# The attention's output projection as three products of split operands, and 18 identity turns in the prologue's waits

## The reference

```
x = x + tanh(g_xattn) * xattn(layernorm(x), ctx, ctx)
x = x + tanh(g_ffn)   * ffn(layernorm(x))

xattn: Q, K, V = x Wq' + bq, ctx Wk' + bk, ctx Wv' + bv      (16 heads of 16)
       out = softmax(Q K' / 4) V, heads side by side (100 x 256)
       return out Wh' + bh
ffn:   rmsnorm, softmax gate over 8 experts, the best 2, SwiGLU of width 1024
       with low-rank deltas of rank 16 for each expert
```

## Time and profile before

| | |
|---|---|
| three timed runs | 498.75, 499.56, 500.44 us; median 499.56 |
| profiled execution | 499.88 us, its span 498.0 us, mean granted clock of TensorE 0.995 |
| TensorE (PE) busy | 97% of the span |
| VectorE (DVE) / ScalarE (ACT) / GpSimd (POOL) busy | 72% / 53% / 56% |
| load of `wh` | issued at 34.2 us, landed 6.3 us later |
| queries of the second chunk split (what `q_l` = 6 counts) | 23.35 us |
| first score head of image 3 | about 69.8 us |
| loads of queries, issue to landing (median) | 3.3 us |
| VectorE, copy of 400 columns out of PSUM (L950) / difference of 400 columns, one operand in PSUM (L884) | 0.57 us / 0.574 us |

### The profile page before, as it was taken

The page is one execution under the profiler, slowest core; times in us unless marked ns, Lnnn a source line. Parts: engine busy times, 40 slices in busy tenths (PEclk is TensorE's granted clock), DMA queues, the critical chain, the costliest instruction groups (busy, mean ns, idle before and its releaser), DMA issues.

```text
span 498.0 us, 11753 instructions
## 1 busy us (share of the span) xinstructions
PE 482.1 (97%) x4350; PEld 454.2 (91%) x4350; DVE 358.4 (72%) x771; ACT 265.7 (53%) x584; POOL 276.9 (56%) x336
## 2 busy tenths in 40 slices
PE   7888999999999999999999999999999999999996
PEld 6657999999999999998999998899999999999994
DVE  5866787888888888988797779745585566764444
ACT  4466766666777766669865532533325333333331
POOL 6545665666666677685434547544485435845440
PEclk9989999999999999999999999999999999999999
DMA  7693786678777676554260000010000100001001
GB/s 214 176 291 98 219 208 163 153 183 195 199 184 180 174 188 158 121 111 79 50 185 1 1 0 2 1 34 1 0 2 0 34 1 1 0 2 34 0 1 33
DMA packets 51144, 45.83 MB, mean 92 GB/s; under 512 B 33935, under 2 KB 40115, under 8 KB 51088
## 3 DMA queue, kind: packets, MB, share of 16 engines
q1 hardware_dynamic: 41310, 23.18, 19.8%
q0 software_dynamic: 7504, 18.69, 14.0%
q10 hardware_dynamic: 2274, 3.21, 2.0%
HBM read 20.59 MB, written 6.66 MB: 55 GB/s over the span
## 4 chain that ended last, share of the span: by engine, by line
PE 90%; DVE 5%; DMA 2%; issue 1%; ACT 1%; SPq 0%; DVEq 0%; ACTq 0%
PE bank L1426 14%; PE bank L1270 9%; PE bank L1293 8%; PE bank L1306 7%; PE bank L1430 7%; PE bank L1443 7%; PE bank L1478 6%; PE bank L1252 6%; PE bank L1240 6%; PE bank L1458 4%; PE bank L1339 3%; PE bank L1461 2%; PE bank L1227 2%; DMA xs<-x 2%; PE bank L1386 2%; PE bank L1318 1%
## 5 line engine op out<-in xcount | busy, mean ns | idle before, releaser
L985 DVE TENSOR_REDUCE nmax<-bank 100x1 f32<-100x361 f32 x256 | 131.1, 530 | 34.0 <-PE bank L1270 29.7
L419 POOL TENSOR_TENSOR awl<-hb,awh 128x400 fp32r<-128x400 f32 x63 | 71.4, 1134 | 119.5 <-ACT awh L623 119.5
L623 ACT ACTIVATE awh<-hb 128x400 fp32r<-128x400 f32 x64 | 34.5, 538 | 118.4 <-DVE hb L921 118.1
L525 ACT ACTIVATE pt<-bank 120x400 f32<-120x400 f32 (+1 forms) x192 | 90.1, 501 | 12.6 <-PE bank L1293 9.5
L1270 PE MATMUL bank<-KS,QS 96*100 96x362 f32 x256 | 86.3, 357 | 3.7 <-DVE nmax L985 2.9
L914 DVE TENSOR_TENSOR hb<-sil,bank 128x400 f32<-128x400 f32 x64 | 36.4, 569 | 71.2 <-PE bank L1443 36.7
L1293 PE MATMUL bank<-QS,KS 97*120 97x200 f32 (+1 forms) x384 | 63.6, 269 | 0.0
L328 POOL TENSOR_TENSOR cth<-craw,cth 128x724 fp32r<-128x724 f32 x16 | 27.7, 1730 | 59.9 <-ACT cth L471 53.6
L1293 PEld LDWEIGHTS bank<-QS,KS 97*120 97x120 f32 (+1 forms) x384 | 59.2, 184 | 0.2
L1270 PEld LDWEIGHTS bank<-KS,QS 96*100 96x100 f32 x256 | 41.6, 167 | 9.6 <-DVE nmax L985 3.3
L333 POOL DMA_DIRECT2D QS<-q_dram x90 | 46.1, 521 | 0.4 <-issue 0.3
(11 more groups left out here) (225 smaller groups left out, 1117.1 us busy)
## 6 DMA issues: line engine op xcount, KB each, us to landing
KS<-kn SPq DMA_DIRECT2D x128, 90.5 KB, 3.3
KS<-kn POOLq DMA_DIRECT2D x64, 90.5 KB, 3.5
craw<-ctxT POOLq DMA_DIRECT2D x14, 361.0 KB, 5.0
QS<-q_dram POOLq DMA_DIRECT2D x92, 50.0 KB, 3.3
q_dram<-qn ACTq DMA_DIRECT2D x4, 400.0 KB, 4.4
o_dram<-on SPq DMA_DIRECT2D x16, 100.0 KB
xr<-o_dram SPq DMA_DIRECT2D x16, 100.0 KB
y<-xs SPq DMA_DIRECT2D x8, 200.0 KB
```

Source lines behind the costliest of these rows:

```text
L419: nc.gpsimd.tensor_tensor(awl[:, g % 2, slot], hb[:, slot], awh[:, g % 2, slot].bitcast(F32), ALU.subtract).then_inc(m["p_awl"], 1)
L525: nc.scalar.activation(pt[0:TW[t], u, :], pT[u % 3][0:TW[t], 0:CS], ACT.Exp, scale=float(DH) ** -0.5).then_inc(m["act_e"], 1)
L985: nc.vector.tensor_reduce(nmax[:, h // 8, pos % 8:pos % 8 + 1], pS[h % 2][0:S, 0:T], AX.X, ALU.max, negate=True).then_inc(m["dve_s"], 1)
```

## The change

The output projection becomes six matmuls of split operands. Its weight is split once, at the end of step 0 (ScalarE the high part, GpSimd the low part); the turned attention output is split each time, the high part by ScalarE (`turned_high`), the low part by VectorE in the place of the copy. In the prologue TensorE turns the identity 18 times at five places, into a bank that `q_proj` overwrites.

```
+        whs = sba("whs", [128, 2, KT, D], F32R)
...
-        ot = sba("ot", [128, KT, S])
+        ots = sba("ots", [128, 2, KT, S], F32R)
...
+                if i == 0:
+                    pool.wait_ge(m["wh_h"], 1)
+                    nc.gpsimd.tensor_tensor(whs[:, 1], wh[:], whs[:, 0].bitcast(F32), ALU.subtract).then_inc(m["wh_l"], 1)
...
+            def turned_high(i):
+                act.wait_ge(m["pe_onT"], i)
+                wait(act, "pe_y", i - 1)
+                nc.scalar.activation(ots[:, 0].rearrange("p k s -> p (k s)"), pP[1][:, 0:KT * S], ACT.Copy).then_inc(m["act_ot"], 1)
...
                 v_out(b, 1)
+                if has_y(i):
+                    turned_high(i)
                 expo(i, 8)
...
                     ctx_high_of(i + 3)
                 if i == 0:
+                    act.wait_ge(m["w_in"], 2 * 16)
+                    nc.scalar.activation(whs[:, 0], wh[:], ACT.Copy).then_inc(m["wh_h"], 1)
                     q_store(2)
...
                 expo(B - 2, 6)
+                turned_high(B - 2)
                 expo(B - 2, 7)
...
                 u_high(0, 0)
+                turned_high(B - 1)
                 u_high(0, 1)
...
                     slot_high(g, 0)
+                if g < 2:
+                    turned_high(B + g)
                 slot_high(g, 1)
...
             def turned_o(i):
-                dve.wait_ge(m["pe_onT"], i)
-                nc.vector.tensor_copy(ot[:].rearrange("p k s -> p (k s)"), pP[1][:, 0:KT * S]).then_inc(m["dve_ot"], 1)
+                dve.wait_ge(m["act_ot"], i)
+                nc.vector.tensor_tensor(ots[:, 1].rearrange("p k s -> p (k s)"), pP[1][:, 0:KT * S],
+                                        ots[:, 0].rearrange("p k s -> p (k s)").bitcast(F32), ALU.subtract).then_inc(m["dve_ot"], 1)
...
             def y_proj(i):
                 wait(pe, "dve_ot", i)
                 if i == 1:
-                    pe.wait_ge(m["w_in"], 2 * 16)
-                for k in range(KT):
-                    last = mm(pP[1][0:S, 0:D], ot[:, k, :], wh[:, k, :], start=k == 0, stop=k == KT - 1)
+                    pe.wait_ge(m["wh_l"], 1)
+                for p in range(3 * KT):
+                    (ho, hw), k = TERMS[p // KT], p % KT
+                    last = mm(pP[1][0:S, 0:D], ots[:, ho, k, :], whs[:, hw, k, :], start=p == 0, stop=p == 5)
                 last.then_inc(m["pe_y"], 1)
...
+            def keep_warm(n):
+                pe.wait_ge(m["q_l"], 3 * KT)
+                for _ in range(n):
+                    nc.tensor.transpose(pT[0][:, 0:128], ident[:], ident[:])
...
             k_proj(1, 0)
+            keep_warm(3)
             s_head(0, 2)
             s_head(0, 3)
             pe.wait_ge(m["dve_kl"], 2)
             k_proj(1, 1)
             s_head(0, 4)
+            keep_warm(4)
             s_head(0, 5)
+            keep_warm(4)
             s_head(0, 6)
+            keep_warm(3)
             turn(4)
             turn(5)
+            keep_warm(4)
             s_head(0, 7)
             q_proj(2, 0)
```

More of the change, by code:

```diff
@@ L187, in program @@
                  "fw_in fw2_in iota_ok erow_s erow_ok tgf_ok g0 g1 nw a_w p_w a_tx pe_t1 a_tth d_ttl pe_g d_lg d_max d_idx d_dm d_ix d_w silu_ok a_th "
-                 "nm_ok pe_u a_uh d_ul pe_ix d_mk p_md pe_w d_wb d_u0 p_u1 pe_h1 pe_h3 a_sil d_hb d_aw a_awh p_awl d_aws a_sh p_sl d_al "
+                 "nm_ok wh_h wh_l act_ot pe_u a_uh d_ul pe_ix d_mk p_md pe_w d_wb d_u0 p_u1 pe_h1 pe_h3 a_sil d_hb d_aw a_awh p_awl d_aws a_sh p_sl d_al "
                  "pe_z d_zt d_zm pe_fy pe_b2 a_fo d_fo pe_out f_out").split()
```

## The result

The changed kernel took 497.18 us (median of 20 executions, 496.33 to 499.39) against 499.45 us (20, 498.08 to 502.34) for the kernel before on the same chip. The ratio is 0.9954, 95% interval 0.9941 to 0.9966: faster by 0.46%. The forecast was 496.6 us, range 495.2 to 498.2. The profiled execution took 496.79 us (span 495.0, mean granted clock 0.999), the one before 499.88 (498.0, 0.995).

What follows compares the result with a forecast made beforehand. The prediction took TensorE, busy 97% of the span, and its clock as the bound. 499.88 - 2.4 (projections) - 1.62 (clock) + 0.22 (turns) + 0.5 (hand-over) = 496.6 us, range 495.2 to 498.2.

Steps and rivals of the forecast that it cites:

- Three products for one: Output projections: six split matmuls take 0.72 us instead of 0.86, 17 times, a gain of 2.4 us.
- Column time: Rival, output projections: six split matmuls take only their columns' time, 0.64 us, 1.3 us less in all, 495.3 us; chance 0.08.
- the four instructions' own price: Bound for the output projections: at 0.215 us each, six matmuls take 1.29 us, a loss of 7.3 us.
- another engine bounds the step: Rival, attention steps: the projections shrink but the gain is lost in a new wait, 499.0 us; chance 0.08.
- High part, low part, halves of `wh`: Operand splits in attention steps, weight split at end of step 0: covered, cost nothing; uncovered 3.2 us (high part), 1.9 (`wh`).
- The hand-over where it is tight: Last attention step and first expert group: the low part, waiting for ScalarE, comes late; +0.2 and +0.3, together +0.5 us.
- The turns: Prologue: 18 turns of 0.109 us, 1.96 us in all, fifteen of them inside TensorE's waits; cost +0.22 us.
- three turns are uncovered, +0.22 us: Prologue: the first three turns delay `k_proj(1, 1)` by 0.33 us and with it ScalarE's `k_high`; +0.22 us.
- The clock: Prologue, 29.40 to 32.80 us: turns hold TensorE's clock, `q_proj(2, 0)` takes 1.38 us instead of 3.00; a gain of 1.62 us.
- no gain from the clock: Rival, prologue: timed runs had no clock loss, or it falls still or elsewhere; only projections count, 497.9 us; chance 0.27.
- The idle stretch is the program's, not chance: Argument against the clock rival: TensorE's idle stretch in the prologue ahead of the fall belongs to the program; no size given.

Runs made afterwards that it cites:

- four-matmul kernel: Changed kernel with four of each output projection's six matmuls, leaving out high part by the weights' low half: 495.10 us, ratio 0.9886 to the kernel before.
- kernel before with early store: Kernel before, with the store of `on` to memory issued behind the second group of key stacks instead of the last: 499.93 us, ratio 0.9996.

## Why the prediction was right, and where its sizes were off

**Three products for one: right.** 0.72 us as the value projection's row said, 17 times. Column time (0.64 for six) is refuted by 102 matmuls, and so is the four instructions' own price. The Trainium skill, "TensorE: Matmul & The Clock Gate", section "Back-to-back issue gap", would have 0.65 for six by columns / 2.4 GHz + 2.5 ns. It gives that gap for an isolated matmul, and says that with a load of weights for every matmul it is too little at few columns and too much at 512. This case's 0.12 us for one, each with its own load, stands above the rule's 0.109. The term, 2.4 us, counted all 17 as taken from the path. One was not: the step of about 200 us is VectorE's, and lasts 13.3 us with six, with four, and with the old ones. That is the rival "another engine bounds the step", true in one step for the 0.14 us. Behind it the distances shrink by 0.12, 0.17, 0.15 and 0.03 us (14.09, 9.93, 9.47 and 13.78 before, 13.97, 9.76, 9.32 and 13.75 with the change, in the two executions named below), and the four-matmul kernel shows that there was little more to be had there.

**High part, low part, halves of `wh`: right.** 0.33 and 0.35 us, both covered; the steps shrink by what the projection does (13.24 to 13.10 in the undisturbed ones). No wait of TensorE for a load of queries or keys stands between 50 and 80 us in a profiled execution with GpSimd's part.

**The hand-over where it is tight: right in place, about right in size.** Predicted +0.5. VectorE's rows of the last attention step and of the first expert group:

```profile
242.46 0.37 DVE L988 TENSOR_TENSOR ots<-bank,ots 128x200 fp32r<-128x200 f32 x1 [0.54 <-ACT ots L621]
...
254.32 0.37 DVE L988 TENSOR_TENSOR ots<-bank,ots 128x200 fp32r<-128x200 f32 x1 [0.35 <-ACT ots L621]
```

VectorE waited for the high part, 0.54 us in the one (0.6 was foreseen) and 0.35 in the other. In the last step it makes TensorE's projection hold the chain for longer:

```profile
242.99 0.85 PE bank L1358 x6
```

That is 0.13 us lost, not 0.2. In the expert stage the `up` of the earlier trace rows shows where the rest goes:

```profile
260.94 1.37 PE bank L1445 x6
```

1.37 us where it held the chain for 1.11; the distance between the last two projections grows from 9.26 to 9.36 us in spite of the shorter one in it, 0.24 lost against the 0.3 taken. What it waited for is what the prediction had named, the silu: the view by source has for these matmuls, between 260 and 262 us, an idle time of 0.2 us that ended with it.

```profile
ACT sil L627: 0.2, 1
```

Together 0.4. The experiment that moved the high part ahead doesn't give this back. It took `up` to 1.22 us and the last step's projection to 0.71, but 0.10 and 0.11 us of the 0.14 and 0.15 came back behind them, as said above. The distance of the last two is 9.31 and 9.30 us there, and 9.36 to 9.40 in the kernels without the move.

**The projections and the hand-over together** can be taken from two undisturbed profiled executions. From the first to the last projection lie 202.23 us in the kernel before with early store (65.06 to 267.29) and 200.55 in the second profile of the change (65.94 to 266.49): 1.68 us, and 0.14 for the last projection itself, which the distance leaves out, 1.8. The sum had 2.4 - 0.5 = 1.9. Of the old 2.4, 0.14 stayed in VectorE's step and 0.4 in the hand-over. It is one execution each. The store's place doesn't matter for it: the third profile of the kernel before has 202.25 us (66.89 to 269.14).

**The turns: their cost was put too high.** The step "three turns are uncovered, +0.22 us" failed: `q_proj(2, 0)` starts where it did, at 29.58 us, in the turns-alone kernel, and in the change 0.16 us later, which is by how much that execution began its work later. So the key part that was to come 0.33 us later didn't push the chain; the way through ScalarE that the prediction laid out from there was not measured piece by piece.

**The clock: the mechanism right, its place in the sum wrong.** The turns hold it, and the loss where it occurs was 1.42 us here (3.00 - 1.58) against the 1.62 that came from comparing with `q_proj(2, 1)`: the first half takes 1.58, not 1.38, at the full clock. But the sum took the profiled execution as the kernel, and its fall as in all executions. The rival had asked whether the timed runs have it, and the answer is: about half (36 of 67 by their mean clock). And 499.88 us was not typical for one with a fall (median 501.21, lowest 499.43): less 1.62 it put the undisturbed kernel at 498.26, whereas these have their median at 499.11. That is 0.85 us too low. With the 0.22 us too high for the turns it makes the 0.6 by which the sum missed: 499.11 - 2.4 + 0.5 = 497.2 us, with 497.14 measured. Put the other way, the sum took 1.62 - 0.22 = 1.40 us from the median for the turns and the clock, and the turns alone took 0.86 (499.77 to 498.91). The measured time lay in the range because the range reached past the case of no gain from the clock, and that case was half true. "The idle stretch is the program's, not chance" was true and didn't suffice: the idle stretch was in every execution, the fall was not. The Trainium skill, "TensorE: Matmul & The Clock Gate", section "What's actually happening", cited for this rival, has the monitor run free of the kernel's start; a fall in five of six profiled executions is in keeping with that and doesn't show it.

So the gain at the median is 1.97 us (499.11 to 497.14) for the projections, in every execution, and some 2.1 us (501.21 less 499.11) in half of the executions for the turns. The turns alone fit: half of 2.1 us is their gain in the mean, 500.10 to 499.00. The change without turns fits less well: 1.5 us in the median of its group, inside its interval, and the eight of its executions with a mean clock of 0.997 or more lie at 498.05, 0.9 above those of the full change. The sorting, which lets falls through there, explains some of it; how much is open. The fall also costs more in the timed executions than in the chains. In these it is 1.3 to 1.7 us, from the start of the turns right ahead of `q_proj(2, 0)` to the end of `q_proj(2, 1)`: 5.72 to 6.09 us in the five with a fall, 4.42 in the one without. The 11 executions with the same mean clock as the first profiled one, 0.995, have their median at 501.28 us, 1.4 above it. Where they lose the rest stays open.

**What stays open besides:** executions of one kernel with an undisturbed clock still lie 2 to 3 us apart (498.08 to 501.12 before, 496.15 to 498.98 with the change). Late transfers are part of it, up to 0.9 us in a step, and a start of work that is up to 0.8 us later; the store's place was tried, with the result told above, the loads behind it were not. How many of the 18 turns are needed, and whether fewer places would do, was not tried either.

## What to carry to other kernels

Writing an fp32 product against resident weights as three products of split operands gained 0.14 us of 0.86 wherever TensorE bounds the step, because two other engines had a third of a microsecond each between the turn and the matmul; price it from the nearest split row of the same columns, and leave out the steps in which another engine holds the chain. Idle time of TensorE ahead of a dense stretch can be filled with dummy turns, here 18 at no cost that the traces show, if they stand inside waits that are there anyway. And before a loss seen in one profile is subtracted from a time, look into how many executions have it. A second and a third profile of the kernel before would not have told: both had the fall. What told was the mean clock of each timed execution.

## What the runs showed of the hardware that was not expected

- The same prologue without turns, with the same idle stretch, kept TensorE's clock in one profiled execution (1.00 from 29 to 33 us, TensorE busy 1.89 of the 3.00 us before) and lost it in five others (0.57 to 0.66 over those 4 us; 0.62 with 1.88 of 3.00 busy), of three kernels that differ only behind it. 18 turns of 0.109 us brought the share of executions with a low mean clock from 50 of 92 to 2 of 83, not to none.
- Split matmuls of 256 columns cost 0.12 us each whether four or six are in a row, and the 0.281 us that the view by source has for one is not its price: six take 0.72.
- A VectorE difference with one operand in PSUM cost what the plain copy had, 0.35 against 0.36 us for 200 columns.
- A small transfer that usually hides, `on` through memory to `xr` or the row of maxima, was late in single steps by 0.3 to 0.9 us, and in other profiled executions, of kernels that issue it at the same place, it was not.
